# Eight-head attention by pairs of batches: keys and queries of two batches in one product

## What is computed

```python
def _layernorm(x, axis=-1, eps=1e-05):
    m = jnp.mean(x, axis=axis, keepdims=True)
    v = jnp.var(x, axis=axis, keepdims=True)
    return (x - m) / jnp.sqrt(v + eps)
...
    def _L1_xattn_ref(x, media, media_mask, ln_g, ln_b, Wq, Wkv, Wo):
...
        HEADS = 8
        DIM_HEAD = 64
...
        xn = _layernorm(x, ln_g, ln_b)
        q = xn @ Wq
        kv = media @ Wkv
        k, v = jnp.split(kv, 2, axis=-1)
...
        q, k, v = (split_heads(q) * scale, split_heads(k), split_heads(v))
        sim = jnp.einsum('bhid,bhjd->bhij', q, k)
...
        sim = jnp.where(media_mask[:, None, None, :], sim, neg_inf)
        attn = jax.nn.softmax(sim, axis=-1)
        out = jnp.einsum('bhij,bhjd->bhid', attn, v)
        out = out.transpose(0, 2, 1, 3).reshape(x.shape[0], x.shape[1], INNER)
        return out @ Wo
```

## Time and profile before

| | us |
|---|---|
| median of 3 runs | 1915.18 (1915.1 to 1916.68) |
| the profiled execution | 1915.71 |
| its span | 1914.0 |
| TensorE busy | 1878.9 (98%) |
| weight loads busy | 1443.8 (75%) |
| DVE busy | 1286.6 (67%) |
| ScalarE busy | 1032.5 (54%) |
| POOL busy | 797.8 (42%) |

### The profile page before, as it was taken

How to read it: one execution, slowest core, us unless ns; L and a number is a source line. 1 busy time by engine, 2 the same in 40 slices (tenths; PEclk the granted TensorE clock), 3 DMA queues, 4 the chain that set the end, 5 groups by cost and what they waited for, 6 DMA issues and landing times.

```text
span 1914.0 us, 42677 instructions
## 1 busy us (share of the span) xinstructions
PE 1878.9 (98%) x13700; PEld 1443.8 (75%) x13700; DVE 1286.6 (67%) x3985; ACT 1032.5 (54%) x2674; POOL 797.8 (42%) x1482
## 2 busy tenths in 40 slices
PE   6999999999999999999999999999999999999999
PEld 5888888888888644444447888888888877788876
DVE  5887877666677678788875565655656566544476
ACT  5767767777777644544444444444444453222243
POOL 3454555656555545655542232222322233222254
PEclk9999999999999999999999999999999999999999
DMA  6334434433443777665663212122121237222131
GB/s 233 135 138 136 135 113 151 156 135 123 146 143 110 136 157 195 172 147 134 140 146 112 79 57 100 67 88 78 55 99 68 76 114 240 99 82 74 66 132 46
DMA packets 221533, 230.32 MB, mean 120 GB/s; under 512 B 123441, under 2 KB 139825, under 8 KB 221377
## 3 DMA queue, kind: packets, MB, share of 16 engines
q1 hardware_dynamic: 221376, 228.42, 39.1%
HBM read 144.47 MB, written 56.64 MB: 105 GB/s over the span
## 4 chain that ended last, share of the span: by engine, by line
PE 89%; DVE 3%; SPq 2%; DMA 2%; issue 2%; POOL 1%; ACT 1%; POOLq 0%; DVEq 0%; ACTq 0%
PE bank L1172 19%; PE bank L1158 18%; PE bank L2739 13%; PE bank L1228 8%; PE bank L1868 8%; PE bank L1243 6%; PE bank L1211 5%; PE bank L1913 4%; PE bank L1148 2%; DMA b_hqT<-b_hq 1%; SPq L1450 1%; PE bank L2636 1%; SPq L1456 1%; PE bank L2778 1%; DVE m_hrow L2555 0%
## 5 line engine op out<-in xcount | busy, mean ns | idle before, releaser
L582 POOL TENSOR_SCALAR a_probs<-a_probs,a_rinv 128x256 f32<-128x256 f32 x512 | 237.4, 482 | 269.6 <-DVE a_rinv L933 269.6
L711 ACT ACTIVATE a_probs<-a_probs,a_negm 128x256 f32<-128x256 f32 x512 | 254.6, 502 | 95.9 <-DVE a_negm L917 94.8
L582 POOL TENSOR_SCALAR c_probs<-c_probs,c_rinv 128x256 f32<-128x256 f32 x128 | 67.0, 533 | 371.6 <-DVE c_rinv L933 371.6
L917 DVE CUSTOM_DVE_ANT_0 a_probs<-bank,a_mbias 128x256 f32<-128x256 f32 x512 | 191.7, 417 | 7.3 <-PE bank L1211 6.6
L2739 PE MATMUL bank<-m_xnT,m_s 128*128 128x512 f32 x768 | 184.4, 391 | 0.0
L926 DVE COPY a_pT<-bank 128x512 f32<-128x512 f32 x128 | 88.3, 690 | 134.8 <-PE bank L1228 134.7
L711 ACT ACTIVATE c_probs<-c_probs,c_negm 128x256 f32<-128x256 f32 x256 | 127.0, 500 | 75.0 <-DVE c_negm L917 75.0
L2739 PEld LDWEIGHTS bank<-m_xnT,m_s 128*128 128x128 f32 x768 | 142.6, 188 | 30.5 <-issue 0.8
L1228 PE MATMUL bank<-a_ident,a_probs 128*128 128x128 f32 x1024 | 154.9, 274 | 4.0 <-ACT a_pT L719 2.3
L1228 PEld LDWEIGHTS bank<-a_ident,a_probs 128*128 128x128 f32 x1024 | 122.0, 141 | 23.6 <-issue 10.8
L1730 ACT ACTIVATE b_hq<-b_hround 128x1024 bf16<-128x1024 f32 x64 | 67.2, 1052 | 123.4 <-POOL b_hround L1669 119.0
(11 more groups left out here) (287 smaller groups left out, 4318.9 us busy)
## 6 DMA issues: line engine op xcount, KB each, us to landing
kept<-a_cT SPq DMA_DIRECT2D x32, 512.0 KB, 5.2
m_ew<-in_L_ffn_w_dram SPq DMA_DIRECT2D x24, 512.0 KB, 8.5
a_cbuf<-in_ctx_dram SPq DMA_DIRECT2D x16, 512.0 KB, 5.6
a_xbuf<-in_x_dram SPq DMA_DIRECT2D x16, 512.0 KB, 4.8
a_resb<-in_x_dram SPq DMA_DIRECT2D x16, 512.0 KB, 4.1
b_part<-in_L_ffn_w_gate_dram SPq DMA_DIRECT2D x32, 256.0 KB, 3.0
b_part<-in_L_ffn_w_up_dram SPq DMA_DIRECT2D x32, 256.0 KB, 4.0
b_part<-in_L_ffn_w_down_dram SPq DMA_DIRECT2D x32, 256.0 KB, 4.3
```

Source lines behind the costliest of these rows:

```text
L582: last = nc.gpsimd.tensor_scalar(pr, pr, rinv[:, s, r:r + 1], 0.0, ALU.mult, ALU.add)
L711: nc.scalar.activation(pr, pr, ACT.Exp, bias=negm[:, s, h % 2, t:t + 1], scale=-1.0, accum_out=ssum[:, s, QT * (h % 2) + t:QT * (h % 2) + ...
L917: nc.vector.tensor_tensor_reduce(out=probs[:, s, h % 2, t], in0=s_bank[h][:, t * SEQ:(t + 1) * SEQ], in1=mbias[:, el.par], scale=-sm_scale ...
```

## The change

Phase c goes by pairs of batches, with four quads to a pair: the even batch's two, then the odd one's. Keys and queries of both batches of the NEXT pair are made in units of one feature row of 128 and 512 tokens: k0 to k3 and q0 to q3, 12 products of 128 x 512 each (the new L1340), where before there were 8 units of 24 products of 128 x 256. STEADY says which units stand in which slot; a "+" behind a name is the next pair, "=" this one and "-" the one before. A number from 0 to 3 behind t, v and o is the 128-token tile of the pair, so tx2, tx3, v2, v3, o2, o3 are the odd batch's. FIRST is the first pair's table: the units k4 to k7 and q4 to q7 are still by batch as before, and its second quad also holds all k0, k1, q0, q1 of the next pair. FINAL is the last pair's: v2, v3, then o of the batch before. tx0 and tx2 stand ahead of the scores in the first and second quad of an even batch.

Queries, keys and turned rows have one buffer for a pair's 512 tokens (`qT`, `kT`, `xnT`), and `contexts` holds both batches' contexts, in two pieces of 256 tokens for each term. A key unit needs both contexts. `load_ahead` loads the next pair's even context, the mask, rows for four batches ahead, and then the odd context, whose buffer is free only when v3 is done. `normalise` of the odd batch of the next pair runs behind the norms of the even batch's first quad, and that of the even one behind those of the odd batch's first quad; `row_stats` runs four batches ahead. Batches 12 and 13 are written out too (AHEAD = 4). Phase m's raw weights lie elsewhere, and their second pair of loads waits for the context buffer, the third for xn.

```diff
+class PairOrder:
...
+    def __init__(self, prologue, first, steady, final, behind, pairs):
+        self.steady, self.pairs = steady, pairs
+        self.order, self.banks = [], {}
+        for i, u in enumerate(prologue):
+            self.put(u, 0, i % 2)
+        for i, (u, ahead) in enumerate(first):
+            self.put(u, ahead, i % 2)
+        for n in range(1, pairs):
+            for i, (u, ahead) in enumerate(steady):
+                if n < pairs - 1 or (u, ahead) in final:
+                    self.put(u, n + ahead, i % 2)
+        for u in behind:
+            self.put(u, pairs - 1, None)
+        self.place = {unit: i for i, unit in enumerate(self.order)}
+
...
-    CUT, AHEAD = (batches // 4, 4) if heads // 4 == 4 else (None, 2)
+    CUT, AHEAD = (batches // 4, 4) if heads // 4 == 4 else (None, 4)
...
+        qT_pair, kT_pair, xnT = [placed(n, [P, 2, KC, 2 * SEQ], F32R) for n in ("qT", "kT", "xnT")]
+        qT, kT = [[t[:, :, :, tokens(par)] for par in range(2)] for t in (qT_pair, kT_pair)]
+        contexts = placed("contexts", [P, 2, 2, KC, SEQ], F32R)
+        resb = [placed(f"resb{i}", [P, QT, DIM]) for i in range(2)]
...
-        SLOTS = [[["tx0", "tx1", "k0a"], ["k0b"], ["q0a", "q0b"], ["o0a", "o0b"]],
-                 [["o1a", "o1b"], ["k1a", "k1b"], ["q1a", "q1b", "v0a"], ["v0b", "v1a", "v1b"]]]
-    BEHIND = ("o0", "o1")
+        STEADY = [[["tx0+", "tx1+", "v2a="], ["v2b="], ["v3="], ["o2-", "o3-"]],
+                  [["tx2+", "tx3+", "k0a+"], ["k0b+"], ["k1+", "q0a+"], ["q0b+", "q1+"]],
+                  [["k2a+"], ["k2b+"], ["k3+"], ["o0=", "o1="]],
+                  [["q2+"], ["q3+"], ["v0+"], ["v1+"]]]
+        FIRST = [[["tx2=", "tx3=", "k6a="], ["k6b="], ["q6="], ["k7="]],
+                 [["q7="], ["v2="], ["v3=", "tx0+"], ["tx1+", "k0+", "k1+", "tx2+", "tx3+", "q0+", "q1+"]],
+                 STEADY[2], STEADY[3]]
+        FINAL = [[["v2a="], ["v2b="], ["v3="], []], [[], ["o2-"], ["o3-"], []], [[], [], [], ["o0="]], [["o1="], [], [], []]]
+    BEHIND = ("o0", "o1") if QUADS == 4 else ("o2", "o3")
...
+    def in_slot(el, q, j):
+
+        if QUADS == 4:
+            return [(u, owner(el, u.rstrip("ab"))) for u in SLOTS[q][j] if exists(el, u.rstrip("ab"))]
+        pair = pair_of(el)
+        quads = {0: FIRST, PAIRS - 1: FINAL}.get(number(pair), STEADY)
+        return [(e[:-1], pair.plus(ahead(e))) for e in quads[2 * el.par + q][j] if e[:-1] != rows_first(el, q)]
...
+    def rows_first(el, q):
+
+        if QUADS == 4 or el.par == 1 or number(el) in (0, batches - 2):
+            return None
+        return ("tx0", "tx2")[q]
...
+        return "q" + str(4 + 2 * el.par + q if number(pair_of(el)) == 0 else 1 + 2 * q), pair_of(el)
...
+        if QUADS == 2 and n < 4:
+            return [n], bias
...
+        def load_ahead(el):
+
+            if el.par == 0 and el.has(2):
+                load_kept(sp, el.plus(2))
+            if el.has(2):
+                load_mask(el.plus(2))
+            if el.has(4):
+                load_rows(el.plus(4))
+            if el.par == 0 and el.has(2):
+                load_kept(sp, el.plus(3))
...
+            load_rows(Element(1, 0, batches))
+            load_rows(Element(1, 1, batches))
...
+    def normed_in(el, q):
+
+        if QUADS == 4:
+            return [el.plus(2)] if q == 1 and el.has(2) else []
+        if number(el) == 0:
+            return [el.plus(2 + q)]
+        return [el.plus(3)] if q == 0 and el.has(3) else []
+
+    def measured_in(el, q):
+
+        if QUADS == 4:
+            return [el.plus(2)] if q == 1 and el.has(2) else []
+        if number(el) == 0:
+            return [el.plus(2 + q)]
+        if number(el) == 1 and q == 0:
+            return [el.plus(3)]
+        return [el.plus(4)] if q == 1 and el.has(4) else []
...
+            fs, _ = feature_rows(u)
+            if len(fs) == 1:
+                if u[0] == "q":
+                    pe.wait_ge(lo_done, units.count(SPLIT, "tx3", el))
+                else:
+                    for par in range(2):
+                        context_ready(pe, Element(el.index, par, batches), None)
+                for k in halves:
+                    for a, b in TERMS:
+                        src = xnT[:, a, k] if u[0] == "q" else contexts[:, :, a, k]
+                        last = nc.tensor.matmul(dst[:] if u[0] == "q" else dst[:].rearrange("p (a n) -> p a n", a=2),
+                                                w[:, b, k, fs[0] * P:(fs[0] + 1) * P], src,
+                                                start=(k == 0 and (a, b) == TERMS[0]),
+                                                stop=(k == KC - 1 and (a, b) == TERMS[-1]))
+                if halves[-1] == KC - 1:
+                    last.then_inc(x_done, 1)
+                return
...
-           for n, places in enumerate(((12, 188), (16, 195), (0, 60)))]
+           for n, places in enumerate(((12, 16), (4, 8), (195, 60)))]
...
+        sp.wait_ge(*prior.gone["context"])
+        load_raw(sp, 1, sw3)
         sp.wait_ge(*prior.gone["xn"])
-        load_raw(sp, 1, sw3)
-        sp.wait_ge(*prior.gone["context"])
...
-    c_places = dict(cT_odd0=0, resb=4, cT=12, cT_odd1=60, xbuf1=80, oT1=20, probs=28, pT=44, oT0=52, qT0=64, kT0=72, xnT=88, xbuf0=96,
-                    wv=116, qT1=100, kT1=108, wk=132, wq=148, wo=164, vb=180, smalls=192, xn=195, mraw=203,
-                    mbias=205)
+    c_places = dict(resb1=0, contexts=4, oT1=20, probs=28, pT=44, oT0=52, xbuf1=60, kT=64, xnT=80, xbuf0=96, qT=100, wv=116,
+                    wk=132, wq=148, wo=164, vb=180, resb0=188, smalls=192, xn=195, mraw=203, mbias=205)
```

More of the change, by code:

```diff
@@ L270, in attention_phase @@
     if prior:
-        PROLOGUE = ["tx0", "k0", "tx1", "q0", "v0", "k1", "q1", "v1"]
-    units = UnitOrder(PROLOGUE, UNITS, BEHIND, batches)
+        PROLOGUE = ["tx0", "k4", "tx1", "q4", "v0", "k5", "q5", "v1"]
+        units = PairOrder(PROLOGUE, listed(FIRST), listed(STEADY), listed(FINAL), BEHIND, PAIRS)
+    else:
+        units = UnitOrder(PROLOGUE, [u for quad in SLOTS for parts in quad for u in finished(parts)], BEHIND, batches)
     NCOLS = sum(b is not None for b in (q_bias, k_bias, v_bias, ln_gain, ln_bias, out_bias))
@@ L364, in turned_context @@
     def turned_context(el, part):
-        return cT_odd[part][:] if prior and el.par == 1 else cT[:, part]
+        return contexts[:, 1 - el.par, part] if prior else cT[:, part]
     def load_weight(sp, name, half=None):
@@ L530, in normalise @@
         if not isinstance(el.n, int) or el.n > 0:
[L531 removed]
+            wait_apart(pool, *last_of("tx", el.plus(-1)))
         mean, var = mv[:, :, 0], mv[:, :, 1]
@@ L621, in iteration @@
                     beside.gpsimd_beside(pool, 2 * quads_left(el, q) + 1)
-                if q == QUADS // 2 - 1 and el.has(2):
-                    normalise(pool, el.plus(2))
+                for ne in normed_in(el, q):
+                    normalise(pool, ne)
                 if q == QUADS - 1 and out_bias is not None:
@@ L1070, in quad_of_8 @@
                 recip(ne, nq, 1)
-            if q == 0 and el.has(2):
-                row_stats(dve, el.plus(2))
+            for ne in measured_in(el, q):
+                row_stats(dve, ne)
         def iteration(el):
```

295 lines of the change are left out of this document (172 added, 123 removed).

## The result

The changed kernel is slower: a median of 1924.17 us (1922.57 to 1930.99, 7 runs) against 1916.86 (1915.1 to 1918.79, 7 runs), ratio 1.0043 with a 95% interval of 1.0033 to 1.0053. The forecast was 1912.1, with no change or a gain as the likely outcomes. Its profiled execution has a span of 1922.4 us, against 1914.0.

The account below looks back on a forecast made before the run. TensorE's gapless list was taken to bound phase c, weight loads pacing 256-column products. The last quad's scores 3.8 us earlier and +0.7 for the raw weight made -3.1: 1912.1 us on the median of 1915.2, range 1905 to 1920.

Parts of the forecast that it names:

- first pair: First pair of phase c: two old waits go, new ones come before k0, tx3 and q0; batch 2 starts at 1105.7.
- six steady pairs: Batches 2 to 13 of phase c: a pair costs 67.19 us, 1.17 less than before, six times.
- the last pair's two quads: End of phase c, little filler: quads of 10.56 and 11.92 us; the last quad's scores start 3.8 us earlier.
- The raw weight: Hand-over to phase m: its second weight loads behind batch 13's store, which waits for o3; +0.7 us (0 to 3).
- phase m behind it: Behind the raw weight, phase m is TensorE's list again and moves as a whole.
- all three waits: First pair, TensorE: 4.4 us (2.5 to 5.7) before k0, about 1.0 at tx3, about 1.6 at q0.
- The gain on a unit: k and q units, 512 columns for 256: 0.03 to 0.18 us saved per unit, 0.16 taken.
- the 66.85 of the prediction: Steady pair: its four quads summed, 17.24, 17.19, 16.26 and 16.16 us, without the wait at tx2; before 68.36.
- The wait at tx2: Head of a steady pair's second quad: TensorE waits 0.34 us (0 to 1.6) for POOL to write the odd batch's xn.
- The rival of a late POOL chain: Steady pairs: POOL's chain to xn is 1.3 us a pair later than summed, giving 1919.9; chance 0.12.
- the two waits of rows 7: First pair: batch 1's scores waited 1.40 us for q, the next quad's T1 1.11; k7 and q7 now stand there.
- the second context of later pairs: Steady pairs: its load after v3 stays hidden, two loads needing 6.8 us against 10.9 us of TensorE work.

Follow-up runs that it names:

- wait_filled: The changed kernel with the four transposes of the second pair's tx1 made ten times in a row just ahead of k0; 1921.23 us, ratio to before 1.0022.
- pairs_256b: The changed kernel with k and q units as 256-column products, the even batch's twelve first, then the odd one's; 1930.57 us, ratio to before 1.0064.
- the kernel both: The changed kernel with another first-pair table, phase m's raw weight issued before batch 13's store, o2, o3 one slot earlier; 1914.74 us, ratio to before 0.9981.

## Why the prediction was wrong

The forecast was 899.1 - 3.1 = 896.0 from the first scores to the end; the changed kernel took 905.0. The 9.0 us between them, by the prediction's steps:

| step | forecast | measured | miss |
|---|---|---|---|
| first pair, from the first scores to the tx0 at the head of batch 2 | 90.8 | 94.2 | +3.4 |
| six steady pairs | 6 x 67.19 | 6 x 67.72 | +3.2 |
| the last pair's two quads | 10.56, 11.92 | 10.94, 11.98 | +0.4 |
| the raw weight | 0.7 | 2.4 | +1.7 |
| phase m behind it | 0 | 0.25 | +0.3 |

The span went up by 8.4 in place of down by 3.1. Of these 11.5 the table has 9.0, and 2.5 are the spread ahead of the first scores. The medians lie 7.3 apart, in the range of the 5.9 and 7.7 of the two profiled executions; that of before went from 1915.18 in the three runs of the prediction to 1916.86 in seven.

**The first pair** is the step that failed in its mechanism: it had no cost for TensorE's low clock behind a wait. It named all three waits, their order and what stands behind them, and came near their lengths: k0 4.4 forecast, 3.37 measured, tx3 1.0 and 0.98, q0 1.6 and 1.50; v3 was done 38.4 us after the first scores by the sum and 38.5 in the trace. Then it priced the work behind them as if it stood behind other work: "k0 and k1 take 5.6", "5.6 for q0, q1". They took 7.15 and 7.07, 3.0 more together. The rest of the 3.4 nearly cancels: k0 starts 0.5 earlier than forecast, the transposes and waits from k1 to q0 take 0.4 more, and the two quads behind 0.4 more. Nothing in the sum nor in a rival stood for a clock that falls. The kernel before, with no wait over 1.40 in phase c, gave no sign of it there. The four executions without the long wait (5.56 to 6.06 for k0 and k1) against the five with it, and wait_filled with its 5.56 at 1.00, show that the wait brings it on. The Trainium skill, TensorE: Matmul & The Clock Gate, section HAM oscillation — how this bites in real kernels, tells of products that start at the low clock behind waits for DMAs. The traces agree in most executions (0.50 behind the 3.37 of the changed kernel) and not in all (1.00 behind the 3.36 of pairs_256b). A rival built on it, two waits and 1.5 us each, would have given 1915.1 and with the raw weight's some 1916.

**The gain on a unit** was mis-sized. 0.16 was taken between bounds of 0.03 and 0.18, and 0.11 is what the width gave. That is 0.40 of the 0.53 that a steady pair misses. The forecast took six products of v at 1.39 from rows 1 and doubled them. But that block stood right behind products of q, with no transposes ahead. The new units stand between transposes, where a half takes 1.47 and a whole one 2.85. The trace of before had that very case, wo between two transposes, and I read past it; TensorE's timeline of before, in the batch of rows 1:

```profile
1246.21 3.01 PE L1158 MATMUL bank<-c_wo,c_oT 128*128 128x512 f32 x12
1249.06 0.60 PE L1228 MATMUL bank<-c_ident,c_probs 128*128 128x128 f32 x4
```

1249.06 - 1246.21 = 2.85. With 2.85 and 1.47 for every block between transposes, v's too, the 66.85 of the prediction become 67.57, and with the wait at tx2 as measured 67.8, against 67.72.

**The wait at tx2**, the difference of two sums of 17, was right within 0.1. It shows on the weight load only, not as an idle product, so TensorE's view of waits alone would have missed it. The weight loads' timeline:

```profile
1129.02 0.42 PEld L1315 LDWEIGHTS bank<-c_ident,c_xn 128*128 128x128 f32 x4 [0.45 <-POOL c_xn L708]
```

From the product before it to tx2's first one is 0.42, where it is 0.23 in front of a tx0 that finds its rows, and the scores start 0.585 behind tx2 and 0.527 behind such a tx0: the wait costs 0.25, forecast 0.34. In pairs_256b it costs 0.27, so the 0.24 of the new order is this wait, a term that the sum had. The quad from S to S was forecast at 17.58 and takes 17.53, in part by luck: v's units were priced too low and o2, o3 too high. The rival of a late POOL chain has fallen.

**The raw weight** came late by the mechanism that the prediction named, the store that now waits for o3 (12.4 us into the quad forecast, 1541.40 - 1528.92 = 12.48 measured). The landing was mis-sized: 4.0, the median of `kept` in rows 6, was taken, and 4.45 us in all. It took 6.4 from the first of the four issues, 1545.23, to the product at 1551.65. The second pair of m_raw's loads has its own line, in before (window 1527 to 1530):

```profile
DMA to landing us min/median/max: 4.7/5.1/5.5
```

and after (window 1545 to 1546):

```profile
DMA to landing us min/median/max: 5.1/5.5/5.9
```

With the 0.44 between the two issues the second was down 6.4 us behind the first issue, and in before it was already 6.0: most of the miss stood in the trace of before, on the tensor itself. The 0.4 more came where the weight's four loads, batch 15's residual rows, the gate's weight and phase m's first rows are issued within 3.3 us, at 305 to 396 GB/s from 1546 to 1556; that this crowding lengthened it is argued, not shown. The wait of 2.98 also took the place of two of before, 0.88 and 0.99. That alone would be in the range of 0 to 3 that the step had; the slow 12 products of wo behind it (3.98 for 2.93) are the clock again. The step's own sum is off by 0.1: 21.14 - 20.56 is 0.6, not 0.7.

**What held:** the gain in the steady pairs is real (0.64 a pair, 3.8 in six), the two waits of rows 7 are gone, the second context of later pairs stays hidden, and no bank or shared buffer shows as a wait of TensorE in the steady pairs. The sign was lost at the ends of the phase: against the 3.8 gained, all that stands up to the last quad outside of the steady pairs costs 7.1 more than before, the hand-over 2.4 and phase m 0.3.

## What to carry to other kernels

A gap on a fully busy TensorE has two prices, its length and the slow products behind it: here 1.0 to 2.9 us on a block of 12 to 48 products behind a single gap of 2.8 to 4.4 us, in most executions but not in all. Price it in the sum whenever a change makes such a gap, and look first whether another order of the same units avoids it; another table for the first pair and another place in SyncE's queue turned 0.4% slower into 0.2% faster. Take a block's price from a row with the same neighbours on both sides, and a landing time from the same tensor, at the load that its queue will then have.

## What the runs showed that I had not expected

- The clock fell behind two waits of 0.98 and 1.50 us with four transposes between them, in five executions of six that have them (q0 and q1 took 7.07 to 7.40 us; in pairs_256b, the sixth, 5.92). In four of the five it had also fallen some 10 us earlier, behind the wait for `kept`; in wait_filled it had not.
- Behind waits of equal length it falls in one execution and stays in the next: 3.36 left k0 and k1 at 5.83 (pairs_256b), 3.37 made them 7.15, and 3.75 made them 7.91. In the kernel both, no gap of phase c had such a price, and its two executions agree to 0.2 us from the first scores on.
- Six products of 512 columns take 1.47 to 1.48 us behind transposes and 1.36 to 1.39 right behind other products (1140.45 to 1141.81 in the changed kernel, rows 1 in before): the neighbours of a block are worth as much as its width.
